# A two-layer graph and expert network on one core: the first layer's slot re-ordered, its routing spread over four slots, and the expert dispatch unrolled

## The chip, the cores and the metric

One Trainium2 chip, one of its cores. The metric is the device time of one execution in microseconds (us). The core has TensorE (PE; its weight loads are listed as PEld), VectorE (DVE), ScalarE (ACT), GpSimd (POOL) and SyncE (SP), which here only issues DMAs.

## The reference, cut to what matters

All numbers are float32. x is 32 batches of 256 nodes with 128 features, adj is 32 x 256 x 256. The change touches the first two of four blocks.

```python
# first graph layer, per batch, H = 4 heads of 32, on n = layernorm(x)
X = lrelu(n @ W_lin + b_lin);  q = lrelu(n @ W_q);  k = lrelu(n @ W_k)
adj_h = adj * sigmoid(q_h @ k_h.T * 32 ** -0.5)          # 256 x 256 for each head
dis   = sum(adj_h, -1) ** -0.5                           # 0 where the degree is 0
x     = x + layernorm(dis * (adj_h @ (dis * X_h))) * ln_g + ln_b
# first expert layer: the two best of 8 experts for each of the 8192 tokens, unweighted
idx = top_k(layernorm(x) @ Wg + bg, 2)
x   = x + sum over the two experts of gelu(n @ W1[e] + b1[e]) @ W2[e] + b2[e]
# then a second graph layer and a second expert layer, which the change leaves as they are
```

## The kernel before

The program is written by hand for all five engines. Every engine runs its own list of instructions in order, and counters (semaphores, `wait_ge`) tie the lists together. Each stage is one function per engine.

**First layer (`gnn0_*`).** A software pipeline over slots `s` from -4 to 40. In slot `s` every engine does a different step for different batches: scores and sigmoid and weighting for batch `s`, keys and queries for `s+1`, transposing x for `s+2`, values for `s-1`, output for `s-2`, and so on back to the gate of the expert layer for `s-6` and `s-7`. The order inside a slot is written out by hand per engine, in the loops at the end of `gnn0_tensor`, `gnn0_scalar`, `gnn0_vector` and `gnn0_gpsimd`.

- PE, per slot: `scores` (L298, 16 matmuls), `transposed_output` (L315), `keys_queries` (L327), `transpose_adj` (L339), `output_rows` (L350), `transpose_x` (L363), `values` (L374, and L375, which adds the bias by a matmul with one row of ones), `transpose_rows` (L387), `degrees` (L398), `gates` (L414), and at the end `transpose_degrees` (L439), which waits for ACT's copy of the degrees (L514).
- ACT: two sigmoids of 1,024 columns (L476), the copies out of PSUM, and last the three normalisations of the slot (L517), for y, x and the rows that go to the experts.
- DVE: two products `adj_h` (L636), the leaky keys and queries (L647), values (L659, L666) and output (L674), six `bn_stats` (L626), the degrees (L679), and a chain of small operations, `solve_steps` (L587 to L620), which finds all reciprocal square roots of the slot: start value, then three Newton steps of three operations (L609, L612, L615), each depending on the last. The other work is put between its links.
- POOL: three additions and products per batch (`add_attention`, L801, L804, L807), then up to four row-scattering DMAs (`send`, L814).

**Routing.** Every fourth slot (10, 14, 18 and so on), DVE picks for four finished batches (1,024 tokens) the two best experts (`choose_steps`, L697 to L724). In the next slot PE counts how many tokens went to each expert before this one: 2 instructions with `before` (L424) and 16 with `ones` (L426), and DVE turns the counts into row numbers (`choose_rows`, L728 to L740). Over the next four slots POOL scatters the 1,024 rows twice (once per chosen expert), 16 indirect DMAs per group, 128 in all. The normalised row carries its token number and the higher expert's rank in two extra columns.

**Dispatch (`ffn0_*`).** When all rows are sent, each expert's rows lie together in DRAM, and 72 blocks of 256 rows are worked off. For each block SP loads the rows (L1004), PE transposes them (L1021), ACT copies (L1076), PE does the hidden layer (L1031), ACT the gelu (L1092), PE the output (L1042), DVE adds the bias (L1158), and POOL scatters the result by token in two indirect DMAs (L1189). DVE also copies the expert's weights to a fixed place (`stage_weights`, L1140) and works out the destinations (L1149, L1152). Which expert a block belongs to is known only at run time, so SP, ACT and DVE read it from memory into a register (`value_load`); DVE does so twice per block. Buffers exist for four blocks. The blocks are done by a loop whose body holds four blocks:

```python
        def over_steps(engine, body):

            body(0, True, False)
            with engine.Fori(1, NBLK // UNROLL - 1) as i:
                body(i, False, False)
            body(NBLK // UNROLL - 1, False, True)
```

SP may load block n+4 when DVE has its destinations (`s_y_at`, `s_higher`) and PE its transposes. DVE does in turn `add_bias(n-2)`, `stage_weights(n+2)`, `destinations(n)`.

Of the kernel before, what the change touches and what calls it, by code (L numbers as in the profile page):

```python
# [41 lines left out]
UNROLL = 4  # L42
DEG_MIN = 2.0 ** -120
RSQRT_MAGIC = float(0x5F3759DF)
# [28 lines left out]
def build_program(nc, I, out):  # L73

    with ExitStack() as ctx:
# [63 lines left out]

        phR = ExitStack()  # L140
# [5 lines left out]
        NROWS = 3  # L146
        rows = sbR("rows", [P, NROWS, GT, ROW])
        xh1T = sbR("xh1T", [P, 2, NN])
        gate = sbR("gate", [P, GT, NE])
# [4 lines left out]
        emask = sbR("emask", [P, GT + 1, NE])  # L154
# [21 lines left out]
        w_k, w_q, w_lin = sb1("w_k", [P, D]), sb1("w_q", [P, D]), sb1("w_lin", [P, D])  # L176
        b_lin = sb1("b_lin", [1, D])
# [17 lines left out]
        AT_X, AT_Y, AT_R = 0, TB, 2 * TB  # L195
        stats = sb1("stats", [P, 2, NLN, 6])
# [3 lines left out]
        rstd = sb1("rstd", [P, 2, NLN + NDEG])  # L200
        shift = sb1("shift", [P, 2, NLN])
        dis = sb1("dis", [P, 2, NDEG])

        s_w1, s_wln = sem("s_w1"), sem("s_wln")
# [3 lines left out]

        s_xhT_ps, s_kq_ps, s_adjT_ps, s_score_ps = sem("s_xhT_ps"), sem("s_kq_ps"), sem("s_adjT_ps"), sem("s_score_ps")
# [4 lines left out]
        s_deg, s_yT, s_yn = sem("s_deg"), sem("s_yT"), sem("s_yn")  # L214
# [4 lines left out]
        s_stats, s_norm, s_dis, s_chA, s_init1 = sem("s_stats"), sem("s_norm"), sem("s_dis"), sem("s_chA"), sem("s_init1")  # L219
# [4 lines left out]
        rank_ps = psum[:, Y_BANK, 0:(GT + 1) * NE]  # L224

        SOLVE_LAG = 3
        FIRST, LAST = -4, NB + 9
# [7 lines left out]
        def solve_no(s):  # L235

            return s + SOLVE_LAG + 1

        def solves(s):
            return batch(s + SOLVE_LAG) or batch(s - 1) or batch(s - 3) or batch(s - 5)  # L240

        def routes(s):

            return s >= 10 and s % GB == 10 % GB and (s - 10) // GB < NG

        def gnn0_sync(sp):
# [20 lines left out]
            for dst, name in ((w_k, "L0_gnn_W_k"), (w_q, "L0_gnn_W_q")):  # L267
                sp.dma_start(dst[:, :], I[name]).then_inc(s_w1, 16)
            load_adj(0)
            sp.dma_start(w_lin[:, :], I["L0_gnn_W_lin"]).then_inc(s_w1, 16)  # L270
            sp.dma_start(b_lin[:, :], I["L0_gnn_b_lin"].rearrange("(a p) -> a p", a=1)).then_inc(s_w1, 16)
            load_x(1)
            load_adj(1)
            for dst, name in ((ln_g, "L0_gnn_ln_g"), (ln_b, "L0_gnn_ln_b")):
                sp.dma_start(dst[:, :], I[name].rearrange("(a n) -> a n", a=1).to_broadcast((P, D)))\
                    .then_inc(s_wln, 16)
            load_adj(2)
            load_gate(sp)
            load_attention3(sp)
            for b in range(NB):  # L280
                if b % 2 == 0 and b // 2 + 2 < NB // 2:
                    load_x(b // 2 + 2)
# [4 lines left out]
        def gnn0_tensor(pe):  # L287
            pe.wait_ge(s_const, 2)
            pe.wait_ge(s_w1, 4 * 16)

# [14 lines left out]
            def transposed_output(b):  # L305
                pe.wait_ge(s_xs, b + 1)
                if b > 4:
                    pe.wait_ge(s_gate, b - 4)
                if b < NB - 4 and b > -4:
                    pe.wait_ge(s_xhT, b + 4)  # L310
                elif b > 0:
                    pe.wait_ge(s_yT, b)
                for c in range(TB):
                    for h in range(HEADS):
                        ins = nc.tensor.matmul(psum[HD * h:HD * (h + 1), YT_BANK, 0:NN],  # L315
                                               xs[:, b % 2, c, HD * h:HD * (h + 1)],
                                               adj_h[:, b % 3, h, c, :], start=(c == 0), stop=(c == TB - 1))
                ins.then_inc(s_yT_ps, 1)

            def keys_queries(b):  # L320
# [122 lines left out]
            for s in range(FIRST, LAST):  # L443
                if batch(s):
                    scores(s)
# [1609 lines left out]
```

## Time and profile before

| | |
|---|---|
| time before, median of 3 runs | 961.0 us (958.96 to 961.82) |
| the profiled execution: its time, its span | 957.8 us, 956.0 us |
| mean granted TensorE clock | 0.856 of full |
| busy: PE, DVE, ACT, POOL | 695.5, 593.8, 431.8, 436.3 us |
| first sigmoid of batch 0, of batch 31 | 18.11 us, 342.48 us |
| first load of an expert block | 436.31 us |
| first and last scatter of expert results | 448.20 us, 692.39 us |

The time is that of the whole execution; the span runs from its first to its last instruction, and every position below is counted from the span's start. Busy shares are means over stages with different limits, so they say little by themselves.

### The profile page before, as it was taken

How to read it: one execution, taken by the hardware profiler on the slowest of the kernel's cores; microseconds unless marked ns; L12 is line 12 of the kernel's file. 1: busy time of each engine (PE TensorE's matmuls, PEld its weight loads, DVE VectorE, ACT ScalarE, POOL GpSimd, SP SyncE). 2: the span in 40 equal slices, each digit the busy share in tenths (PEclk: the TensorE clock that was granted, in tenths of full speed). 3: DMA queues.
4: the chain of work that ended last, by engine and by line, in shares of the span. 5: the costliest groups of instructions: out<-in, count | busy, mean ns of one | idle time of the engine just before them, and what ended most of it. 6: DMA issues, size and time to landing. Idle time of an engine off the chain costs nothing. (4 is left out here: it accounts for less than half of the span.)

```text
span 956.0 us, 18424 instructions
## 1 busy us (share of the span) xinstructions
PE 695.5 (73%) x4886; PEld 543.5 (57%) x4886; DVE 593.8 (62%) x2480; ACT 431.8 (45%) x1018; POOL 436.3 (46%) x478
## 2 busy tenths in 40 slices
PE   3989798888888885405776667676546774699994
PEld 2556565555555553404665556665446673589993
DVE  6898978787878767331333333333267784348898
ACT  4576665565655533103333333332212556567771
POOL 0022245554555557762555555545644310185540
PEclk9998998997898865556889999898768997699998
DMA  7223123222221111822222222222199940102211
GB/s 186 82 63 89 56 78 100 78 80 78 79 78 57 45 35 35 245 87 68 77 77 72 72 83 77 76 72 78 56 216 214 175 110 1 46 1 68 68 36 53
DMA packets 90507, 79.97 MB, mean 84 GB/s; under 512 B 11025, under 2 KB 79810, under 8 KB 89410
## 3 DMA queue, kind: packets, MB, share of 16 engines
q1 hardware_dynamic: 69250, 54.84, 20.5%
q0 software_dynamic: 21184, 24.27, 10.5%
q8 instruction: 33, 0.54, 0.2%
q14 instruction: 40, 0.33, 0.1%
HBM read 46.39 MB, written 32.69 MB: 83 GB/s over the span
## 5 line engine op out<-in xcount | busy, mean ns | idle before, releaser
L1189 POOL DMA_INDIRECT expert_outputs<-y_rows,y_at x144 | 138.5, 962 | 120.8 <-DVE y_rows L1158 77.9
L814 POOL DMA_INDIRECT expert_rows<-rows,row_of x128 | 125.6, 981 | 45.3 <-issue 34.3
L1158 DVE TENSOR_TENSOR y_rows<-psum,f_b 128x256 f32<-128x256 f32 x72 | 30.6, 425 | 124.9 <-PE psum L1042 71.2
L801 POOL TENSOR_TENSOR y_n<-y_n,ln_g 128x256 f32<-128x256 f32 x32 | 23.4, 732 | 185.6 <-ACT y_n L517 185.3
L1092 ACT ACTIVATE hT<-psum,f_b 128x256 f32<-128x256 f32 x144 | 60.5, 471 | 87.6 <-remote 36.7
L1021 PE MATMUL psum<-ident,xin 128*128 128x128 f32 x144 | 33.6, 319 | 90.2 <-DMA xin<-expert_rows 87.8
L1031 PE MATMUL psum<-xinT,wst 128*128 128x256 f32 x288 | 88.2, 434 | 12.1 <-DVE wst L1140 9.9
L1042 PEld LDWEIGHTS psum<-wst,hT 128*128 128x128 f32 x576 | 83.0, 208 | 7.6 <-issue 2.8
L1042 PE MATMUL psum<-wst,hT 128*128 128x128 f32 x576 | 83.2, 292 | 2.5 <-DVE y_rows L1158 2.5
L636 DVE TENSOR_TENSOR adj_h<-psum,adjT 128x1024 f32<-128x1024 f32 x64 | 77.8, 1216 | 9.4 <-ACT psum L476 6.4
L1076 ACT ACTIVATE xinT<-psum 128x256 f32<-128x256 f32 x72 | 27.7, 385 | 116.4 <-PE psum L1021 89.4
L1021 PEld LDWEIGHTS psum<-ident,xin 128*128 128x128 f32 x144 | 17.8, 156 | 99.9 <-issue 69.6
L476 ACT ACTIVATE psum<-psum 128x1024 f32<-128x1024 f32 x64 | 61.3, 994 | 19.4 <-PE psum L298 16.4
L1031 PEld LDWEIGHTS psum<-xinT,wst 128*128 128x128 f32 x288 | 55.3, 213 | 23.5 <-issue 12.6
L1733 PEld LDWEIGHTS psum<-w2s,hT 128*128 128x128 f32 x512 | 61.8, 192 | 4.6 <-ACT hT L1777 2.2
L1715 PE MATMUL psum<-xh3T,w1s 128*128 128x256 f32 x256 | 62.7, 389 | 2.3 <-DVE w1s L1841 1.9
L1733 PE MATMUL psum<-w2s,hT 128*128 128x128 f32 x512 | 62.7, 275 | 2.1 <-DVE xh L1860 2.1
L315 PE MATMUL psum<-adj_h,xs 128*32 128x256 f32 x512 | 44.9, 480 | 22.7 <-issue 20.0
L1324 PE MATMUL psum<-hf,adjT 128*128 128x130 f32 x256 | 38.5, 321 | 23.4 <-issue 13.6
L1140 DVE TENSOR_SCALAR wst<-f_w 128x512 f32 x72 | 32.4, 450 | 33.9 <-issue 33.7
L1777 ACT ACTIVATE hT<-psum,b1sel 128x256 f32<-128x256 f32 x128 | 50.1, 470 | 5.9 <-PE psum L1715 5.8
L1935 POOL COPY w1s<-f_w 128x256 f32 x60 | 24.9, 424 | 60.9 <-issue 32.6
(250 smaller groups left out, 1656.7 us busy)
## 6 DMA issues: line engine op xcount, KB each, us to landing
xin<-expert_rows SPq DMA_DIRECT2D x72, 130.0 KB
adj_in<-in_adj_dram SPq DMA_DIRECT2D x32, 256.0 KB, 3.8
adjT_scratch<-adjT SPq DMA_DIRECT2D x32, 256.0 KB, 3.0
adjT<-adjT_scratch SPq DMA_DIRECT2D x8, 1024.0 KB
xres<-expert_outputs POOLq DMA_DIRECT2D x12, 512.0 KB, 11.3
xres<-in_x_dram SPq DMA_DIRECT2D x16, 256.0 KB, 3.5
out_dram<-yout SPq DMA_DIRECT2D x6, 512.0 KB, 3.1
expert_outputs<-y_rows,y_at POOLq DMA_INDIRECT x144
```

Source lines behind the costliest of these rows:

```text
L315: ins = nc.tensor.matmul(psum[HD * h:HD * (h + 1), YT_BANK, 0:NN], xs[:, b % 2, c, HD * h:HD * (h + 1)], adj_h[:, b % 3, h, c, :], start=( ...
L476: nc.scalar.activation(pair, pair, ACT.Sigmoid, scale=float(HD) ** -0.5).then_inc(s_att, 1)
L636: nc.vector.tensor_tensor(adj_h[:, b % 3, 2 * u:2 * u + 2, :, :].rearrange("p h c n -> p h (c n)"), psum[:, 2 * u:2 * u + 2, :], adjT[:, b ...
L814: pool.indirect_dma_start(rows_dram[:, :], bass.IndirectOffsetOnAxis(ap=row_of[:, g % 3, k, t:t + 1], axis=0), rows[:, g % 3, t, :], None) ...
L1021: ins = nc.tensor.transpose(psum[:, u % 2, r * P:(r + 1) * P], xin[:, u, r, 0:D], ident[:, :])
L1031: ins = nc.tensor.matmul(psum[:, 2 + u, c * SLOTS:(c + 1) * SLOTS], wst[:, u, c * P:(c + 1) * P], xinT[:, u, :], start=True, stop=True)
L1042: ins = nc.tensor.matmul(psum[:, 6 + u % 2, r * P:(r + 1) * P], hT[:, u, c, r * P:(r + 1) * P], wst[:, u, HID + c * D:HID + (c + 1) * D], ...
L1092: ins = nc.scalar.activation(hT[:, u, c, :], psum[:, 2 + u, c * SLOTS:(c + 1) * SLOTS], ACT.Gelu, bias=f0_b1[:, bass.ds(e * FC + c, 1)])
L1189: pool.indirect_dma_start(y_dram[:, :], bass.IndirectOffsetOnAxis(ap=y_at[:, u, r:r + 1], axis=0), y_rows[:, u, r, :], None).then_inc(s_y_ ...
L1715: ins = nc.tensor.matmul(psum[:, 2 * (n % 2) + k, c * NN:(c + 1) * NN], w1s[:, n % SLOTS4, k, c * P:(c + 1) * P], xh3T[:, n * NN:(n + 1) * ...
L1733: ins = nc.tensor.matmul(psum[:, 4 + n % 2, r * P:(r + 1) * P], hT4[:, n % 2, k, c, r * P:(r + 1) * P], w2s[:, n % SLOTS4, k, c * D:(c + 1 ...
L1777: nc.scalar.activation(hT4[:, n % 2, k, c, :], psum[:, 2 * (n % 2) + k, c * NN:(c + 1) * NN], ACT.Gelu, bias=b1sel[:, c, k, n:n + 1]).then ...
```

## The change

It has these parts.

1. **The slot's order** is new on all engines. PE transposes the degrees of batch s-1 after the scores of batch s, and does gates and the adjacency transposes before the keys. ACT puts `normalise_y` between the two sigmoids, and normalises y, x and rows with the numbers solved one slot earlier (`s - 1`), so `rstd`, `shift` and `dis` have three sets in place of two; x is normalised for batch s+3 from statistics taken for batch s+5. The pipeline starts one slot earlier (-5). DVE weighs the values of batch s-2, early in the slot.
2. **Newton**: two steps in place of three, the second one written as a cubic; 8 operations with the start value in place of 10.
3. **Value bias**: the weights are centred once (`w_c = w - mean`), the transposed x gets +1 from ACT's bias, and the bias row is folded into `w_c`, so the matmuls of L375 go.
4. **Routing**: `choose_steps` and the new `place_steps` are spread by single steps over the following slots, and the counting is two matmuls on prefix sums (`upto`) that DVE makes. The last group of four batches is split in two. Sending starts at slot 14. The token column is written by ACT.
5. **Dispatch**: no loop; all 72 blocks are written out. The output bias travels with the staged weights (640 columns in place of 512), so `add_bias` needs no `value_load`; the destinations are one operation, and result rows lie in pairs per token.

```diff
-        SOLVE_LAG = 3
-        FIRST, LAST = -4, NB + 9
+        FIRST, LAST = -5, NB + 9
+        ROUTES = [(GB * g, GB) for g in range(NG - 1)] + [(NB - GB, GB // 2), (NB - GB // 2, GB // 2)]
...
+            nc.tensor.matmul(psum[:, 0, 0:3 * D], ones[:, :], w_all[:, :, :].rearrange("p k d -> p (k d)"),
+                             start=True, stop=False)
+            nc.tensor.matmul(psum[:, 0, 2 * D:3 * D], ones[0:1, :], b_neg[:, :], start=False, stop=True)\
+                .then_inc(s_wc_ps, 1)
...
+            def rank(g, s):
+                nc.tensor.matmul(rank_ps[:, 0:(tiles + 1) * NE], ones[:, :],
+                                 upto[:, 0:tiles + 1, :].rearrange("p t e -> p (t e)"), start=True, stop=False)
+                nc.tensor.matmul(rank_ps[:, 0:tiles * NE], before[:, :],
+                                 emask[:, 4:4 + tiles, :].rearrange("p t e -> p (t e)"), start=False, stop=True)\
+                    .then_inc(s_rank_ps, 1)
...
             for s in range(FIRST, LAST):                      # PE
                 if batch(s):
                     scores(s)
+                if batch(s - 1):
+                    transpose_degrees(s - 1)
+                ranked = ranks(s)
+                if ranked is not None:
+                    rank(ranked, s)
+                if batch(s - 7):
+                    gates(s - 7)
+                if batch(s + 1):
+                    transpose_adj(s + 1)
+                    keys_queries(s + 1, ranked)
                 if batch(s - 2):
                     transposed_output(s - 2)
+                if batch(s - 1):
+                    values(s - 1, ranked)
+                if batch(s + 2):
+                    transpose_x(s + 2)
                 if batch(s - 2):
                     output_rows(s - 2)
                 if batch(s):
                     degrees(s)
                 if batch(s - 6):
+                    transpose_rows(s - 6)
...
             for s in range(FIRST, LAST):                      # ACT
                 if batch(s):
                     sigmoid(s, 0)
+                if batch(s - 4):
+                    normalise_y(s - 4, s - 1)
+                if batch(s):
                     sigmoid(s, 1)
...
+                if batch(s - 6):
+                    normalise_rows(s - 6, s - 1)
+                if batch(s + 3):
+                    normalise_x(s + 3, s - 1)
...
+            for s in range(FIRST, NB + 14):                   # POOL
                 if batch(s - 4):
                     add_attention(s - 4)
+                if batch(s - 14):
+                    send(*parts[s - 14])
...
-        def over_steps(engine, body):
-            body(0, True, False)
-            with engine.Fori(1, NBLK // UNROLL - 1) as i:
-                body(i, False, False)
-            body(NBLK // UNROLL - 1, False, True)
+        def over_blocks(body):
+            for n in range(NBLK):
+                body(n, n % UNROLL, n // UNROLL)
...
-                nc.vector.tensor_scalar(higher[:, u, :], xin[:, u, :, D + 1], expert_rank[:, bass.ds(n, 1)],
-                                        float(NT * P), ALU.is_gt, ALU.mult).then_inc(s_higher, 1)
-                dve.wait_ge(s_higher, n + 1)
-                nc.vector.tensor_tensor(y_at[:, u, :], xin[:, u, :, D], higher[:, u, :], ALU.add).then_inc(s_y_at, 1)
+                nc.vector.scalar_tensor_tensor(y_at[:, u, :], xin[:, u, :, D + 1], expert_rank[:, n:n + 1],
+                                               xin[:, u, :, D], ALU.is_gt, ALU.add).then_inc(s_y_at, 1)
...
+            for n in range(NBLK):                             # DVE
+                if n > 1:
+                    add_bias(n - 2)
+                destinations(n)
+                if n + 2 < NBLK:
+                    stage_weights(n + 2)
```

## Rows read from the trace of the kernel before

**Rows 1.** Windows: stage, length, busy PE, PEld, DVE, ACT, POOL, clock, DMA, GB/s.

```profile
18.11:104.95 86.84, 75.32 (x678) 47.24 (x682) 77.22 (x288) 56.61 (x116) 14.40 (x20) 0.92 0.29 87
104.95:342.48 237.53, 202.22 (x1684) 132.41 (x1676) 192.12 (x747) 137.31 (x291) 120.19 (x139) 0.89 0.24 74
342.48:436.31 93.83, 38.34 (x189) 27.80 (x189) 43.49 (x213) 14.37 (x33) 61.08 (x67) 0.52 0.33 99
...
448.20:693.36 245.16, 170.88 (x972) 146.43 (x970) 82.17 (x278) 80.25 (x205) 138.51 (x144) 0.91 0.25 74
693.36:956.00 262.64, 192.47 (x1297) 177.24 (x1297) 184.55 (x870) 130.79 (x350) 100.40 (x96) 0.88 0.40 90
```

**Rows 2.** Timeline of ACT: sigmoids of batches 11, 12, 13, 16, 17.

```profile
114.64 1.90 ACT L476 ACTIVATE psum<-psum 128x1024 f32<-128x1024 f32 x2
129.85 1.92 ACT L476 ACTIVATE psum<-psum 128x1024 f32<-128x1024 f32 x2 [2.93 <-PE psum L298]
138.90 1.91 ACT L476 ACTIVATE psum<-psum 128x1024 f32<-128x1024 f32 x2
...
172.99 1.93 ACT L476 ACTIVATE psum<-psum 128x1024 f32<-128x1024 f32 x2 [2.36 <-PE psum L298]
184.45 1.91 ACT L476 ACTIVATE psum<-psum 128x1024 f32<-128x1024 f32 x2
```

**Rows 3.** Timeline of DVE and POOL, one slot, from 58.20 us.

```profile
58.20 0.73 POOL L801 TENSOR_TENSOR y_n<-y_n,ln_g 128x256 f32<-128x256 f32 x1 [6.32 <-ACT y_n L517]
58.45 0.52 DVE L587 TENSOR_TENSOR msum<-stats 128x6 f32<-128x6 f32 x1
59.02 0.73 POOL L804 TENSOR_TENSOR y_n<-y_n,ln_b 128x256 f32<-128x256 f32 x1
59.15 0.61 DVE L592 SCALAR_TENSOR_TENSOR mdiff<-mdiff 128x6 f32<-128x6 f32 x1
59.89 0.68 DVE L595 SCALAR_TENSOR_TENSOR veps<-sqsum,mdiff 128x6 f32<-128x6 f32 x1
...
67.11 0.51 DVE L587 TENSOR_TENSOR msum<-stats 128x6 f32<-128x6 f32 x1
```

**Rows 4.** DVE's groups by shape, 60 to 340 us.

```profile
L615 DVE SCALAR_TENSOR_TENSOR rstd<-newt,rstd 128x14 f32<-128x14 f32 x78 | 12.6, 162 | 0.7
...
L685 DVE TENSOR_TENSOR gate<-psum,f_bg 128x16 f32<-128x16 f32 x24 | 3.9, 162 | 0.0
L717 DVE TENSOR_TENSOR emask<-hot 128x64 f32<-128x64 f32 x5 | 3.8, 769 | 0.2
...
L728 DVE TENSOR_TENSOR pos<-psum,filled 128x64 f32<-128x64 f32 x5 | 1.1, 225 | 8.4 <-PE psum L426 8.4
```

**Rows 5.** Timeline at the end of the sending: POOL's last scatter, SP's first loads.

```profile
433.12 0.96 POOL L814 DMA_INDIRECT expert_rows<-rows,row_of  x1 [0.30 <-issue]
...
436.31 3.67 SPq L1004 DMA_DIRECT2D xin<-expert_rows  x4
```

**Rows 6.** DVE's groups by shape, dispatch, 448 to 694 us.

```profile
L1140 DVE TENSOR_SCALAR wst<-f_w 128x512 f32 x68 | 30.5, 449 | 31.1 <-issue 31.1
L1158 DVE TENSOR_TENSOR y_rows<-psum,f_b 128x256 f32<-128x256 f32 x71 | 30.2, 425 | 118.1 <-PE psum L1042 64.3 <-issue 30.5 <-remote 23.3
L1149 DVE TENSOR_SCALAR higher<-xin,expert_rank 128x2 f32<-128x2 f32 x70 | 16.0, 229 | 4.4 <-issue 3.8 <-DMA expert_outputs<-y_rows,y_at 0.6
```

**Rows 7.** Timeline of DVE, dispatch: three successive bias additions.

```profile
524.53 0.42 DVE L1158 TENSOR_TENSOR y_rows<-psum,f_b 128x256 f32<-128x256 f32 x1 [0.76 <-issue]
...
529.82 0.42 DVE L1158 TENSOR_TENSOR y_rows<-psum,f_b 128x256 f32<-128x256 f32 x1 [2.75 <-PE psum L1042]
...
532.13 0.42 DVE L1158 TENSOR_TENSOR y_rows<-psum,f_b 128x256 f32<-128x256 f32 x1 [0.67 <-issue]
```

**Rows 8.** POOL's waits, 448 to 694 us: total, times, longest.

```profile
POOL expert_outputs L1189 <- DVE y_rows L1158: 77.9, 26, 14.1
```

**Rows 9.** DMA queue that fetches instructions, 18 to 383 us: packets, MB, share.

```profile
q8 instruction: 21, 0.34, 0.4%
```

More of the change, by code:

```diff
@@ new lines, in gates @@
+            def gates(b):
+                pe.wait_ge(s_xh1T, b + 1)
+                if b + 8 < NB:
+                    pe.wait_ge(s_xhT, b + 9)
+                elif b + 4 < NB:
+                    pe.wait_ge(s_yT, b + 5)
+                elif b > 0:
+                    pe.wait_ge(s_gate, b)
+                if b == 0:
+                    pe.wait_ge(s_w2, W2_LOADS)
+                    pe.wait_ge(s_const2, CONST2)
+                for t in range(TB):
+                    ins = nc.tensor.matmul(psum[:, YT_BANK, t * NE:(t + 1) * NE], xh1T[:, b % 2, t * P:(t + 1) * P],
+                                           f0_wg[:, :], start=True, stop=True)
+                ins.then_inc(s_gate_ps, 1)
@@ L430, in transpose_degrees, with values @@
-            def transpose_degrees(b, ranked):
+            def values(b, ranked):
+                if ranked is not None and b + 2 >= NB:
+                    pe.wait_ge(s_ranked, ranked + 1)
+                elif b + 2 < NB:
+                    pe.wait_ge(s_raw, b + 3)
+                elif b > 0:
+                    pe.wait_ge(s_xd, b)
+                for t in range(TB):
+                    ins = nc.tensor.matmul(psum[:, KQ_BANK, t * P:(t + 1) * P], xhT[:, b % 4, t * P:(t + 1) * P],
+                                           w_c[:, 2, :], start=True, stop=True)
+                ins.then_inc(s_X_ps, 1)
@@ L744, in gnn0_vector @@
                 steps = solve_steps(s) if solves(s) else iter(())
-                picks = choose_steps((s - 10) // GB) if routes(s) else iter(())
+                late = s >= NB
+                next(steps, None)
+                if s == FIRST + 1:
+                    dve.wait_ge(s_wc_ps, 1)
+                    nc.vector.scalar_tensor_tensor(
+                        w_c[:, :, :].rearrange("p k d -> p (k d)"), psum[:, 0, 0:3 * D], -1.0 / D,
+                        w_all[:, :, :].rearrange("p k d -> p (k d)"), ALU.mult, ALU.add).then_inc(s_wc, 1)
+                if batch(s - 2):
+                    weigh_values(s - 2)
+                next(picks, None)
+                if batch(s - 2):
+                    leaky_values(s - 2)
                 next(steps, None)
@@ L1033, in hidden, with output @@
                 ins.then_inc(s_bh_ps, 1)
-            def output(i, u, first):
-                n = UNROLL * i + u
+            def output(n):
+                u = n % UNROLL
                 pe.wait_ge(s_bh, n + 1)
-                if not (first and u < 2):
+                if n > 1:
                     pe.wait_ge(s_y_rows, n - 1)
@@ L1179, in ffn0_vector @@
[L1179 to L1193 removed]
+            stage_weights(0)
```

703 lines of the change are left out of this document (357 added, 346 removed).

## The prediction

> **What bounds the kernel now.** I read the windows by stage first, then the timeline of one slot, then the groups and waits of the two stages that the change touches.
>
> The first layer takes 86.84 us for slots 0 to 9 and 237.53 us for slots 10 to 30; its tail and the rest of the sending take 93.83, the dispatch 245.16 and all that follows 262.64 [rows 1]. The first two stages belong to DVE: it is busy 77.22 of 86.84 us, and in slot 5 it issues without a gap, from one start of its chain (58.45) to the next (67.11), 8.66 us [rows 3]. From slot 10 on DVE is busy only 192.12 of 237.53 us [rows 1]. The loss sits in the routing. An ordinary slot takes 138.90 - 129.85 = 9.05 us; the slot with the counting takes 129.85 - 114.64 = 15.21, and the one after it, seen in the next group, 184.45 - 172.99 = 11.46 [rows 2].
>
> The tail is POOL's. One scatter costs 0.96 + 0.30 = 1.26 us [rows 5]; after the additions of the last batch 36 are still to be sent, and SP loads the first block 2.2 us after the last one ends (434.08 to 436.31) [rows 5].
>
> In the dispatch POOL has 2 x 1.26 = 2.52 us of work per block. The stage takes 245.16 / 72 = 3.41 us per block, and POOL waits 77.9 us in it for the biased rows [rows 1, 8]. DVE in its turn is idle 118.1 us before adding the bias [rows 6]. Its fastest round is 532.13 - 529.82 = 2.31 us, and the round before that took 5.29 [rows 7]. So the block rate is POOL's pace plus bubbles in a ring of four buffers, where DVE at 2.31 us is hardly faster than POOL and can't catch up after one.
>
> **The change part by part.** The sum is made against the profiled execution, 957.8 us with a span of 956.0; it lies 3.2 us under the median of 961.0, which I add at the end.
>
> *A slot of the first layer.* I start from slot 5 (8.66 us), which has no statistics of finished rows and no gates. Those are two `bn_stats` and one small operation, an estimate of 0.5 us from the spacing of such operations: 9.2 us, which the ordinary slot's 9.05 agrees with. From this go:
>
> - POOL's three operations. DVE's small operations at 58.45, 59.15 and 59.89 take 0.52, 0.61 and 0.68 us, and each of the first two ends where POOL's operation ends (58.93, 59.75) [rows 3]. Undisturbed such an operation takes 0.16 [rows 4]. That is 0.36 + 0.45 + 0.52 = 1.3 us per slot. The change starts POOL's batch after ACT's first sigmoid, when DVE is in the two 1.2 us products whose one input is in PSUM. No row shows a product against a POOL operation; the nearest is the gate addition, also from PSUM, which lies at that place in the slot and still takes 162 ns [rows 4]. So I take the delay as gone, with 0 and 1.3 us as bounds.
> - Two links of the Newton chain, 0.2 us each from start to start where nothing is between them (0.16 to 0.17 of it busy) [rows 4]: 0.4 us.
>
> That leaves 7.5. The PE work removed (bias matmuls, 16 of the counting instructions) I cost at nothing inside the slot: DVE covers it. It matters where DVE waited for the counts, 8.4 us in five groups [rows 4], which I count as gone, since the two matmuls come early in the slot and DVE has the values to weigh meanwhile.
>
> Routing adds 20 DVE operations per group in place of 21. Back to back one costs about 0.25 us, in the shadow of the chain's links 0.14; 4.0 us per group, 1.0 per slot, bounds 0.7 and 1.3. Some of them stood beside POOL at 769 ns each [rows 4] and no longer do. Slot: 8.5 us without a wait.
>
> DVE idles 45.4 us in slots 10 to 30 [rows 1]; without the counts' 8.4 that is 37, or 1.8 per slot. PE no longer ends its slot by waiting for ACT's degrees, which takes the wait for them; the delay after the start of a new group's scatters (the 11.46 us slot) I can't place, and leave. I keep half: 0.9. The slot comes to 9.4 us, bounds 8.5 and 10.3. Slots 10 to 30: 21 x 9.4 = 197 against 237.5, **-40 us** (-59 to -21).
>
> *Slots 0 to 9.* Six of them have POOL's 1.3, all have the 0.4: 11.8 us, if all of it counts. The first slots wait for ACT and PE instead (9.6 us idle in the stage [rows 1]), so **-8 us** (-12 to 0).
>
> *The start.* Three weights, the bias, a matmul and one DVE operation now precede the first keys, and DVE's first wait is for all four loads. I see about two DMA issues and one matmul more ahead of the first sigmoid: **+1.5 us** (0 to +3).
>
> *The tail.* Sending begins two slots later, so after the last addition 44 scatters are left, not 36: 8 x 1.26 = 10 us more. What it gives back: the routing of the last groups no longer holds up the slots before it, and POOL no longer waits for the last rows, as the last group is half as large. POOL's own work from slot 31 on is five batches of 3 x 0.81 us and 60 scatters of 1.26, 88 us; with about 1.5 us until slot 31's rows, 1.5 more as that slot is longer than POOL's work in it, and the 2.2 us at the end, 93 us. Before it is 93.8: **-1 us** (-4 to +5). This is the queue to watch: everything else in the tail (experts' weights, row table, padding) is hidden behind POOL's 44 scatters, 55 us.
>
> *The dispatch.* DVE's round loses one `value_load` (0.75 us, an estimate from the idle stretches of rows 6 and 7: 0.76 us before the bias addition) and one of two destination operations with its wait (0.26); the weight copy grows by 640/512 of 449 ns, +0.11 [rows 6]. 2.31 becomes 1.4 us, well under POOL's 2.52. PE, ACT and SP lose their register arithmetic. Destinations are now ready before the weight copy, so SP's next load starts about 0.9 us sooner. POOL is then the bound at 2.52, and the question is how much of the remaining 0.89 us per block stays as bubbles. The late bias additions (5.29 us) come from waits whose cause I can't see; with a ring of four at POOL's pace (10.1 us) and some 8 us of latency from load to bias, part of each is absorbed. I take 2.9 us per block: 72 x 0.51 = **-36 us** (bounds 2.6 and 3.3: -58 to -8). Nothing after the dispatch changes in work: 262.64 us stay [rows 1].
>
> Sum: -40 - 8 + 1.5 - 1 - 36 = -83.5; 961.0 - 83.5 = 877.5, say 877 us.
>
> **Two rules beside this.** The trace shows DVE's small operations ending with POOL's [rows 3]. The Trainium skill, SBUF — State Buffer, Who interferes with whom, gives the cause: an operation with two inputs in SBUF needs a port that POOL holds exclusively, one with a PSUM input does not. By that rule the products are free, but the leaky keys and the routing steps, with two SBUF inputs, could be hit at their new places; this is the rival on the port below. On unrolling, the same skill's Runtime: NRT & Kernel Launch, Instruction fetch mechanics, says that a sequencer refills in 16 KiB blocks ahead of need and that a taken branch outside its window stalls; here the loop's body is small, so that rule alone gives the unrolling little.
>
> **Rivals.**
>
> 1. *Bubbles stay.* If the delays in the dispatch hit POOL's own supply chain whatever DVE's pace, the block stays at 3.4 us. For it: DVE's waits are longest for PE, whose work per block is unchanged. Against: DVE's fastest round is now slower than needed to catch up. 877 + 36 = 913 us.
> 2. *POOL at its floor and slots without waits.* 2.6 us per block and slots of 8.8: 877 - 22 - 13 = 842 us. POOL's even scatters in the tail [rows 5] speak for the floor.
> 3. *The port.* POOL's third operation, or all three, falls on DVE operations with two SBUF inputs: 0.5 us in each of 31 slots, 893 us. For it: the products cover only 2.3 us and POOL's work of 2.4 starts later than they do.
> 4. *The order gains nothing.* PE now puts the keys behind the values' weighing and the counts (`s_xd`, `s_ranked`), and behind the keys stand the output, values, x and degrees. If this chain takes the time that the routing left, the slots stay at 11.3 us and only the dispatch gains: 877 + 48 = 925 us.
> 5. *Slower.* 72 blocks written out must be fetched: PE alone has some 32 instructions per block. If each of about 20 extra fetches stopped an engine that all wait for, it would take 84 / 20 = 4.2 us each to cancel the gain; at 5 us each the time is 977. Against: 21 such fetches lie in the first layer [rows 9], where DVE issues without a gap for a whole slot [rows 3].
>
> **How the numbers follow.** Forecast 0.42 (its own range 855 to 905), rival 1 0.20, rival 2 0.16, rival 3 0.08, rival 4 0.07, rival 5 0.05, no gain anywhere 0.02. The range reaches to rivals 2 and 4: 838 to 926. A measurement of this kernel tells a change from none at about 0.3%, 3 us: faster 0.93, within that 0.02, slower 0.05.
>
> **What would show it.** First sigmoids of batches 12 to 30 evenly 9.4 us apart, with no slot over 12; DVE's L587, L592, L595 counterparts at 0.16 to 0.17 us; no wait of DVE for the counts over 1 us; batch 31's sigmoid near 296 us, the first block load near 389, POOL issuing without a gap over the 44 scatters before it. In the dispatch, scatters 1.26 us apart for long runs and a stage near 209 us. The prediction is wrong if the slots wait for PE's keys, if POOL still waits over 40 us in the dispatch, or if the tail grows by the 10 us of its extra scatters.

## The result, and the profile after

The changed kernel takes 926.1 us (923.5 to 929.2, 4 runs), the kernel before beside it 961.4: a ratio of 0.9635 (0.9598 to 0.9673). It is faster by 35 us where I had forecast 84, and lies at the very top of my range, 0.1 us above its 926. Its profiled execution has a span of 924.7 us. Windows by stage of the changed kernel (columns as in rows 1):

```profile
20.89:92.39 71.50, 62.43 (x639) 39.20 (x640) 67.14 (x262) 56.88 (x114) 13.47 (x18) 1.00 0.35 106
92.39:316.79 224.40, 175.21 (x1536) 109.97 (x1536) 168.95 (x710) 139.21 (x295) 114.93 (x131) 0.87 0.23 73
316.79:425.78 108.99, 27.30 (x143) 18.00 (x143) 44.18 (x233) 16.10 (x39) 69.59 (x75) 0.52 0.29 90
...
437.00:661.05 224.05, 160.86 (x976) 143.28 (x974) 72.98 (x208) 81.20 (x205) 143.22 (x144) 0.92 0.30 82
661.05:924.70 263.65, 193.36 (x1297) 177.93 (x1297) 184.45 (x870) 130.90 (x350) 100.69 (x97) 0.87 0.40 89
```

| stage, us | before | after | change | forecast |
|---|---|---|---|---|
| start, to the first sigmoid | 18.11 | 20.89 | +2.8 | +1.5 |
| slots 0 to 9 | 86.84 | 71.50 | -15.3 | -8 |
| slots 10 to 30 | 237.53 | 224.40 | -13.1 | -40 |
| tail, to the first block load | 93.83 | 108.99 | +15.2 | -1 |
| first load to first result scatter | 11.89 | 11.22 | -0.7 | 0 |
| dispatch | 245.16 | 224.05 | -21.1 | -36 |
| rest | 262.64 | 263.65 | +1.0 | 0 |

Three stages miss by 27, 16 and 15 us to one side, one by 7 to the other. In slots 10 to 30 DVE has less work than before (168.95 us for 192.12 [rows 1]) and yet is idle for 55.5 us, where it was idle for 45.4. Where does that idle time lie? DVE's groups by shape, 60 to 310 us, changed kernel (busy, mean ns, idle before and what ended it):

```profile
L642 DVE SCALAR_TENSOR_TENSOR mdiff<-mdiff 128x6 f32<-128x6 f32 x25 | 13.5, 539 | 0.0
...
L637 DVE TENSOR_TENSOR msum<-stats 128x6 f32<-128x6 f32 x25 | 4.2, 170 | 3.3
L744 DVE TENSOR_SCALAR veps<-psum 128x8 f32<-128x8 f32 x25 | 4.1, 164 | 25.1 <-PE psum L479 20.7 <-remote 4.3
...
L817 DVE TENSOR_TENSOR pos<-psum,filled 128x64 f32<-128x64 f32 x5 | 1.1, 215 | 0.0
```

The wait for the counts is gone (L817; 8.4 us before [rows 4]). In its place stand 25.1 us before the degrees (L744), for PE. The timeline around one change of slot shows why PE is late. It is the changed kernel's, from 226 us:

```profile
226.34 0.69 PE L479 MATMUL psum<-ident,deg 128*128 128x128 f32 x2 [2.86 <-ACT deg L555]
227.06 0.17 DVE L744 TENSOR_SCALAR veps<-psum 128x8 f32<-128x8 f32 x1 [2.82 <-PE psum L479]
...
228.38 0.85 POOL L914 TENSOR_TENSOR y_n<-y_n,ln_g 128x256 f32<-128x256 f32 x1 [3.70 <-ACT y_n L558]
228.56 0.69 DVE L642 SCALAR_TENSOR_TENSOR mdiff<-mdiff 128x6 f32<-128x6 f32 x1
...
229.25 2.34 DVE L700 TENSOR_TENSOR adj_h<-psum,adjT 128x1024 f32<-128x1024 f32 x2
...
234.45 0.44 PE L454 MATMUL psum<-ident,rows 128*128 128x128 f32 x2
...
236.95 0.38 ACT L549 ACTIVATE xh1T<-psum 128x256 f32<-128x256 f32 x1 [1.89 <-remote]
237.23 0.38 ACT L555 ACTIVATE deg<-psum 128x256 f32<-128x256 f32 x1
237.49 1.03 ACT L515 ACTIVATE psum<-psum 128x1024 f32<-128x1024 f32 x1
```

PE ends the transposes of the rows (L454) at 234.89. ACT has nothing else to do and waits for them, but copies them (L549) only at 236.95: the increment by which PE tells ACT arrives 2.0 us after the work that it reports. Behind it stand ACT's copy of the degrees, PE's transpose of them (L479), DVE's next step and the next sigmoid. In the slots that send rows, the profile puts 28.8 us of ACT's idle time before L549 down to "remote", that is, to no work of an engine. The group of L549, changed kernel, 127 to 317 us:

```profile
L549 ACT ACTIVATE xh1T<-psum x17: 372/384/385, 134.0 to 315.2; 128x256 f32<-128x256 f32 x17
its engine sat idle before it (us, times) until:
  remote: 28.8, 11
```

The trace also holds the increments one by one, so the delay can be read without the idle times. In the slots before the scatters each stands at most 0.07 us behind the end of the instruction that makes it, most of them 0.01 us. In slots 10 to 30 of the changed kernel 73 increments stand more than 0.5 us behind the last instruction that could have made them, up to 3.5 us, all of them PE's and all later than the first scatter (131.91 us). In its dispatch there are 110, up to 4.0 us, all PE's. The kernel before has them too: 38 in slots 10 to 30 and 108 in the dispatch. After the last scatter of the dispatch neither kernel has one. Such an increment is called late below.

The tail shows the same on other engines. Timeline of the changed kernel, 398 to 426 us:

```profile
398.25 24.65 SPq L1103 DMA_DIRECT2D expert_rows<-pad_rows  x8
...
401.79 0.17 DVE L1217 COPY end_b<-end_a 128x2 f32<-128x2 f32 x1 [2.57 <-remote]
...
404.61 0.36 DVE L1217 COPY end_a<-end_b 128x4 f32<-128x4 f32 x1 [2.59 <-remote]
...
410.64 1.15 POOL L930 DMA_INDIRECT expert_rows<-rows,row_of  x1 [0.30 <-issue]
...
425.78 0.41 SPq L1113 DMA_DIRECT2D xin<-expert_rows  x1
```

POOL sends its last row at 410.64, without one gap in the 44 scatters, as forecast. But SP needs 24.65 us to issue eight padding transfers (9.17 us in the kernel before), and goes on to the first load only 14 us after POOL's end. Until 417.5 us one instruction of SP starts every 1.4 us, so the effect outlasts POOL's last scatter (over at 411.79) by 5.8 us. Even DVE's steps that wait only for DVE's own last step begin up to 2.6 us after it.

In the dispatch it is DVE that waits for PE again. POOL's waits for DVE, 73.7 and 1.9 us, look like the 77.9 before [rows 8], but both totals hold the wait for the first block, which ends where the stage begins: 25.2 us after and 14.1 before. Inside the stage POOL waits 50.4 us for DVE where it waited 63.8, and 30.5 us between its own instructions (`issue`) where it was 42.8. That is 25.7 us less, beside 4.7 us more of scattering (143.22 for 138.51), and makes the stage's 21 us. (The line names the destinations, `y_at`; those of a block are long ready then, and it is the result rows of L1255 that end the wait.) DVE's and POOL's waits, changed kernel, 437 to 661 us (total, times, longest):

```profile
DVE y_rows L1255 <- PE psum L1151: 86.2, 34, 3.5
DVE y_rows L1255 <- issue: 17.5, 10, 2.6
```

```profile
POOL expert_outputs L1277 <- DVE y_at L1249: 73.7, 43, 25.2
POOL expert_outputs L1277 <- issue: 30.5, 100, 0.3
POOL expert_outputs L1277 <- DVE y_rows L1255: 1.9, 1, 1.9
```

### The profile page after: what moved, and what is told of

Read it like the earlier page. It is cut to its first block and busy times, and to the rows that moved or that the text cites. A ratio compares the mean times of both kernels' runs of the same rounds, so it can differ in the third digit from the quotient of the medians.

```text
span 924.7 us, 16632 instructions
## 1 busy us (share of the span) xinstructions
PE 636.0 (69%) x4654; PEld 500.0 (54%) x4654; DVE 554.2 (60%) x2375; ACT 436.6 (47%) x1026; POOL 443.6 (48%) x478
## 3 DMA queue, kind: packets, MB, share of 16 engines
q0 software_dynamic: 21184, 24.27, 11.2%
## 5 line engine op out<-in xcount | busy, mean ns | idle before, releaser
L1277 POOL DMA_INDIRECT expert_outputs<-y_rows,y_at x144 | 143.7, 998 | 106.0 <-DVE y_at L1249 73.7
L1140 PE MATMUL psum<-xinT,wst 128*128 128x256 f32 x288 | 84.8, 421 | 54.0 <-issue 46.4
L914 POOL TENSOR_TENSOR y_n<-y_n,ln_g 128x256 f32<-128x256 f32 x32 | 25.4, 794 | 170.6 <-ACT y_n L558 170.6
L1255 DVE TENSOR_TENSOR y_rows<-psum,wst 128x256 f32<-128x256 f32 x72 | 30.4, 422 | 118.9 <-PE psum L1151 92.0
L700 DVE TENSOR_TENSOR adj_h<-psum,adjT 128x1024 f32<-128x1024 f32 x64 | 75.0, 1212 | 0.4 <-ACT psum L515 0.3
L515 ACT ACTIVATE psum<-psum 128x1024 f32<-128x1024 f32 x64 | 64.3, 1010 | 14.5 <-PE psum L334 9.7
L1130 PE MATMUL psum<-ident,xin 128*128 128x128 f32 x144 | 30.6, 298 | 46.6 <-DMA xin<-expert_rows 46.3
L408 PE MATMUL psum<-xhT,w_c 128*128 128x256 f32 x128 | 46.7, 500 | 16.5 <-DVE xd L725 15.7
L2024 POOL COPY w1s<-f_w 128x256 f32 x60 | 24.9, 426 | 59.0 <-issue 30.5
L1804 PEld LDWEIGHTS psum<-xh3T,w1s 128*128 128x128 f32 x256 | 47.3, 195 | 8.0 <-DVE w1s L1930 2.1
L1240 DVE TENSOR_SCALAR wst<-f_w 128x640 f32 x72 | 36.2, 503 | 25.2 <-issue 24.9
```

The costliest lines, as they stand in the source:

```text
L408: ins = nc.tensor.matmul(psum[:, KQ_BANK, n * NN:(n + 1) * NN], w_c[:, n, :], xhT[:, b % 4, :], start=True, stop=True)
L515: nc.scalar.activation(pair, pair, ACT.Sigmoid, scale=float(HD) ** -0.5).then_inc(s_att, 1)
L700: nc.vector.tensor_tensor(adj_h[:, b % 3, 2 * u:2 * u + 2, :, :].rearrange("p h c n -> p h (c n)"), psum[:, 2 * u:2 * u + 2, :], adjT[:, b ...
L1140: ins = nc.tensor.matmul(psum[:, 2 + u, c * SLOTS:(c + 1) * SLOTS], wst[:, u, c * P:(c + 1) * P], xinT[:, u, :], start=True, stop=True)
L1277: pool.indirect_dma_start(y_dram[:, :], bass.IndirectOffsetOnAxis(ap=y_at[:, u, r:r + 1], axis=0), y_rows[:, u, r, :], None).then_inc(s_y_ ...
L1804: ins = nc.tensor.matmul(psum[:, 2 * (n % 2) + k, c * NN:(c + 1) * NN], w1s[:, n % SLOTS4, k, c * P:(c + 1) * P], xh3T[:, n * NN:(n + 1) * ...
```

## The experiments

Twelve kernels ran in four calls, on three chips; the kernel before ran beside each, and its time turned out to be the first finding.

| call | chip | before, us | kernels |
|---|---|---|---|
| 1 | Q | 876.9 (870.2 to 884.1) | e1, e2, e3, e4 |
| 2 | R | 951.7 (942.3 to 953.9) | e5, e6 |
| 3 | R | 950.1 (946.0 to 955.3) | e7, e8, e9, e10 |
| 4 | S | 956.9 (1 run) | e11, e12 |

**e1_sp_early**, on chip Q, adds one wait in `store_adjT`:

```diff
                 sp.wait_ge(s_adjT, b + 1)
+                sp.wait_ge(s_att, 2 * b + 1)
```

> The changed kernel with one more wait on SP: the store and the load of an adjacency go out only after the first sigmoid of the next slot, when POOL does its additions and no scatter is under way. In the changed kernel the slots 14 to 31 take 11.1 us each, and in them PE's increments reach ACT 2 to 4 us late just after SP has issued its transfers among POOL's scatters. Theory A (the transfers beside the scatters hold the increments up): the late increments go, these slots fall to about 9 us, and the kernel gains some 30 us. Theory B (the scatters alone hold them up): slots stay at 11 us, total within 5 us of 926. Theory C (the new order of the slot is itself 11 us long): no change of the slots either, and PE's increments may come in time without anything being gained.

832.3 us, 0.948 of before (0.939 to 0.956). The slots 14 to 30 take 8.70 us each. That looks like theory A; it is not, as e4, which lacks this edit, and e6 show.

**e2_send_last**, on chip Q, moves all `send` calls behind the loop over the slots and has nine row buffers.

> The changed kernel with nine row buffers, and POOL sends no row before all 32 batches have been added: the slots run without a scatter, and 128 scatters of 1.26 us (161 us) follow them. Read are the slots 14 to 31 alone; the total must rise by about 60 to 70 us. If scatters hold up the signals (theories A and B), these slots take 8.1 to 8.6 us, as slots 10 to 12 do in the changed kernel, and no increment of PE comes late. If the new order is 11 us long by itself (theory C), they stay near 11 us.

932.1 us, one run; slots 14 to 30 at 8.4 us each. On this chip it tells nothing of late increments, as the slots with scatters (e1, e4) take no more than 8.7 and the 128 scatters behind the slots make none late either. It is repeated as e11.

**e3_before_unrolled**, on chip Q, is the kernel before with

```diff
-            body(0, True, False)
-            with engine.Fori(1, NBLK // UNROLL - 1) as i:
-                body(i, False, False)
-            body(NBLK // UNROLL - 1, False, True)
+            for i in range(NBLK // UNROLL):
+                body(i, i == 0, i == NBLK // UNROLL - 1)
```

> The kernel before with its 72 blocks written out and nothing else changed: DVE keeps both register reads and both destination operations. My prediction gave the unrolling itself nothing and the thinner DVE round 36 us. If that holds, the dispatch stays at 3.4 us per block (245 us) and the total at 961. If the loop's register arithmetic on all engines was the brake, the block falls towards the 3.1 us of the changed kernel and the total to about 940. If fetching the written-out code costs, it is slower than 961.

876.0 us, 0.996 of before (0.990 to 1.002): unrolling alone gives nothing. Windows of it: slots 0 to 9, slots 10 to 30, tail, dispatch, rest.

```profile
18.06:103.66 85.60, 73.09 (x678) 46.65 (x682) 76.72 (x288) 56.68 (x116) 14.40 (x20) 0.94 0.29 90
103.66:321.42 217.76, 190.60 (x1684) 127.56 (x1676) 189.17 (x746) 136.97 (x290) 119.72 (x139) 0.93 0.26 80
321.42:407.48 86.06, 35.39 (x189) 25.77 (x189) 45.16 (x214) 14.25 (x34) 60.66 (x67) 0.56 0.36 108
...
419.15:604.70 185.55, 150.17 (x972) 132.63 (x970) 87.75 (x278) 83.52 (x205) 139.61 (x144) 0.98 0.33 99
604.70:871.85 267.15, 196.68 (x1297) 181.13 (x1297) 184.78 (x870) 131.01 (x350) 100.80 (x97) 0.85 0.39 88
```

Its dispatch runs at 185.55 / 72 = 2.58 us per block, close to POOL's 2.52, with the thick DVE round of 2.31 us that I had blamed.

**e4_wide_rows**, on chip Q, loads a block in longer pieces; its first layer is the changed kernel's, line for line.

```diff
-  rows_dram[bass.ds(at, SLOTS), :].rearrange("(t p) d -> p t d", p=P)
+  rows_dram[bass.ds(at, SLOTS), :].rearrange("(p t) d -> p t d", p=P)
```

> The changed kernel, but a block's load gives each partition two neighbouring rows (1,040 bytes in a piece) in place of two rows 128 apart (520 bytes each): the same bytes in half as many pieces; which row lies in which partition does not matter, as each row carries its token. If the number of pieces in flight beside the scatters makes the stretches in which no increment arrives (three of about 1.2 us in every three blocks), the block falls from 3.1 us towards 2.8 and the total by about 20 us. If the scatters alone make them, or the time of the load doesn't matter, it stays within 3 us of 926.

830.2 us, 0.946 of before (0.937 to 0.955). Windows of the same stages:

```profile
20.44:91.69 71.25, 61.98 (x639) 39.05 (x640) 67.10 (x262) 56.84 (x114) 13.46 (x18) 1.00 0.35 107
91.69:272.87 181.18, 158.25 (x1531) 99.93 (x1532) 167.51 (x709) 139.16 (x295) 114.22 (x129) 0.95 0.28 89
272.87:366.44 93.57, 25.10 (x149) 17.54 (x149) 45.13 (x235) 16.09 (x39) 71.18 (x77) 0.57 0.34 107
...
377.40:561.75 184.35, 148.36 (x976) 131.37 (x974) 77.48 (x208) 83.44 (x205) 140.75 (x144) 0.99 0.34 100
561.75:826.90 265.15, 194.87 (x1297) 179.37 (x1297) 184.85 (x870) 130.77 (x350) 99.73 (x97) 0.87 0.40 89
```

The group of L549 in it, 125 to 273 us, no longer knows a "remote":

```profile
L549 ACT ACTIVATE xh1T<-psum x17: 371/383/384, 131.8 to 271.8; 128x256 f32<-128x256 f32 x17
its engine sat idle before it (us, times) until:
  PE psum L454: 2.6, 8
```

DVE's idle time in slots 10 to 30 is 13.7 us, not 55.5. On chip Q no increment of any engine comes late, in any stage of e1 to e4. Whether the edits or the chip did that, the next call tells.

**e5_after_again**, on chip R, is the changed kernel itself.

> The changed kernel itself, unchanged, beside the kernel before on the chip of this call. In the runs on record so far the kernel before took 961 us in the first measurement and 877 beside the first four experiments, and there no increment of PE came late, with or without scatters. Theory S (the late signals belong to the chip or to what runs beside it, not to the kernel): where the kernel before takes about 877, the changed one takes about 832, its dispatch stands at 2.55 us per block like that of the kernel before, and the slots 14 to 31 at 8.8; where the kernel before takes about 961, the changed one takes 926 with late increments. Theory K (the earlier load and the shifted transfers of the other experiments removed them): 926 either way, with late increments in its trace.

908.6 us, 0.958 of before (0.950 to 0.965); 212.57 us for slots 10 to 30, 219.55 for the dispatch, late increments throughout. With e1 to e4 that speaks for theory S. That theory names the chip or what runs beside the kernel; with one call on Q and two on R the runs can't tell these two apart.

**e6_both**, on chip R, joins the edits of e1 and e4.

> The changed kernel with both edits of the first call: adjacency transfers after the slot's first sigmoid, and a block's load in pieces of 1,040 bytes. On a chip where no increment comes late I expect no difference from the changed kernel (within 3 us), since the dispatch stands at POOL's 2.55 us per block and the slots wait for no transfer. On a chip where they come late, this is the first run of either edit there: by theory A (transfers beside scatters make it) the slots fall from 11.1 to about 9 us and the block from 3.1 to about 2.8; by theory B (nothing of the kernel's transfers matters) neither moves.

918.5 us, 0.965 of before (0.957 to 0.973): no better than e5. Windows of e6, slots 10 to 30 and dispatch:

```profile
92.37:310.26 217.89, 175.93 (x1536) 108.68 (x1536) 168.15 (x710) 139.21 (x296) 115.00 (x131) 0.87 0.25 76
428.90:648.50 219.60, 160.73 (x976) 143.29 (x974) 73.58 (x208) 81.07 (x205) 142.81 (x144) 0.93 0.29 84
```

Theory A falls, for both edits: neither another place for SP's transfers of the adjacency nor a load in fewer pieces makes the slots or the blocks faster.

**e7_ring6**, on chip R, with `RING = 6`; the result rows and destinations (`y_rows`, `y_at`) get six buffers too:

```diff
-        xin = sb2("xin", [P, UNROLL, SLOTS // P, ROW])
+        xin = sb2("xin", [P, RING, SLOTS // P, ROW])
...
-                    sp.wait_ge(s_y_at, n - UNROLL + 1)
+                    sp.wait_ge(s_y_at, n - RING + 1)
```

> The changed kernel with six buffers in place of four for the rows that come in, the result rows and their destinations; weights, hidden layer and PSUM banks stay at four. Where signals come late in the dispatch, POOL then has up to two more blocks of results to scatter while nothing arrives: if the stretches without a signal (4 to 6 us in every 9.4 us) are only ridden out in the ring, the block falls from 3.05 us to about 2.7 and the total by 20 to 25 us. If each stretch also stops POOL's own supply whatever lies in the ring (my rival 1), it stays at 3.0 to 3.1. Where no signal comes late, nothing changes: 2.55 us per block.

913.8 us, 0.959 of before (0.954 to 0.965), beside 0.962 for e10: no difference. The block takes 3.06 us, 3.05 in e10. More room for loads and for results gains nothing. That leaves the handovers between PE, ACT, PE and DVE as the place where the time goes, each made by an increment; the buffers between those (weights, hidden layer, PSUM) stayed at four, and no run tried more of them.

**e8_send_first**, on chip R, puts `send` ahead of `add_attention` in POOL's slot.

> The changed kernel, POOL doing the four scatters of a slot ahead of the three additions instead of behind them. The same scatters fall in the first half of the slot, under DVE's products and PE's keys, and the signals at the slot's end (degrees, rows) go out when no scatter is under way. Where signals come late: if only those at the end of the slot cost time, since each of PE, ACT, PE, DVE then waits for the last, the slots 14 to 31 fall from 10.5 or 11 us to about 9.5. If any four scatters cost the slot 2.5 us wherever they lie, they stay. Where none comes late: slots at 8.8 us, unless POOL's additions, now later, hold up the rows' statistics (then up to 1 us more per slot).

920.1 us, 0.969 of before (0.966 to 0.971). Slots 10 to 30 take 224.24 us against 212.01 in e10, and DVE still waits 25.0 us for the degrees from 140 to 310 us. Moving the scatters helps nothing: 75 increments come late in its slots 10 to 30, 63 in e10's.

**e9_before_unrolled_again**, on chip R, is e3 once more.

> The kernel before with only its 72 blocks written out, once more, in the hope of a chip on which signals come late (the first run of it met none: 2.57 us per block). There it separates the two parts of the dispatch: if DVE's thinner round is what brought the block from 3.39 to 3.05 or 3.11 us, this kernel stays at 3.4; if unrolling did, it is at 3.1. Where no signal comes late, 2.57 again.

948.6 us, 0.998 of before (0.994 to 1.001). Unrolling gives nothing here either. The dispatch in the windows of e9:

```profile
443.37:681.00 237.63, 167.17 (x972) 146.65 (x970) 81.45 (x278) 80.62 (x205) 137.62 (x144) 0.90 0.27 78
```

**e10_after_third**, on chip R, is the changed kernel as the measure for the three above.

> The changed kernel unchanged, as the measure for the other three on this chip. With the kernel before at about 877 I expect 831 here, dispatch 2.55 us per block, slots 10 to 30 in about 181 us and no late signal; with the kernel before at 950 to 961, 908 to 926.

914.5 us, 0.962 of before (0.957 to 0.967). Slots 10 to 30 and the dispatch in the windows of e10:

```profile
91.94:303.95 212.01, 169.78 (x1536) 106.67 (x1536) 165.31 (x710) 139.03 (x296) 115.83 (x131) 0.90 0.25 78
...
421.96:641.60 219.64, 157.73 (x976) 140.43 (x974) 73.01 (x208) 80.89 (x205) 143.35 (x144) 0.94 0.30 84
```

237.63 against 219.64: where increments come late, what the change does to the dispatch beside unrolling it is worth 18 us. DVE's thinner round is the largest part of it by my costs; no run separates it from the earlier destinations and loads.

**e11_send_last_again**, on chip S, is e2 once more.

> The changed kernel with all scatters after the slots, once more (the first run of it met no late signal at all and its slots 18 to 30 took 8.5 us). On a chip where signals come late (the kernel before at 945 us or more): if they need scatters in flight, the slots 10 to 30 again take 178 us in place of the changed kernel's 212 to 224, and late increments appear only once the scatters begin. If the transfers of the adjacency alone are enough on such a chip, the slots stay near 10 us.

974.0 us, one run, beside 956.9 for the kernel before. Slots 10 to 30 in its windows:

```profile
92.07:270.36 178.29, 158.32 (x1531) 99.63 (x1532) 165.15 (x709) 138.56 (x295) 46.93 (x63) 0.95 0.22 67
```

178.29 us, and not one late increment before the scatters begin at 303.5 us; from there to the first load there are 24, and in its dispatch, which scatters, 108 (219.79 us). So the order of the slot is not what takes 10 to 11 us.

**e12_plain**, on chip S, sends the same rows to fixed places, and loads the blocks and writes their results at fixed places too. It leaves out the sorting by expert, so it computes something else.

```diff
-                    pool.indirect_dma_start(
-                        rows_dram[:, :], bass.IndirectOffsetOnAxis(ap=row_of[:, g % NROWS, k, t:t + 1], axis=0),
-                        rows[:, g % NROWS, t, :], None).then_inc(s_sent[g % NROWS], 16)
+                    pool.dma_start(rows_dram[at:at + P, :], rows[:, g % NROWS, t, :])\
+                        .then_inc(s_sent[g % NROWS], 16)
```

> The changed kernel with every scatter of POOL replaced by a plain transfer of the same 128 rows from the same queue to a fixed place; blocks are loaded from fixed places as well. It leaves out the sorting of the rows, so the rows that the experts see and the order of their results are others. Both stages run with the same bytes, loads and instructions on PE, ACT and DVE. On a chip where signals come late: if the scattered addresses or the per-row descriptors that POOL writes for them make the signals late, they vanish here, the slots fall to about 8.5 us and the block to 2.5 us or less, since POOL's plain issue is shorter than 1.26 us. If any write from POOL's queue beside SP's transfers does it, slots and blocks keep their 10.5 and 3.05 us.

769.4 us, one run, beside 956.9. Slots 10 to 30, tail and dispatch in its windows:

```profile
93.38:271.98 178.60, 158.07 (x1531) 99.29 (x1532) 165.00 (x709) 138.86 (x296) 83.05 (x131) 0.95 0.32 92
271.98:348.16 76.18, 25.43 (x149) 17.64 (x149) 44.75 (x235) 16.10 (x39) 42.94 (x75) 0.55 0.59 129
359.36:505.35 145.99, 139.69 (x976) 130.23 (x974) 72.95 (x208) 83.58 (x205) 86.58 (x144) 1.00 0.45 126
```

No increment is late in any stage, on the chip where e11, in the same call, has them from its first scatters on. Each of the two kernels ran there once. POOL's transfers go through the same queue in the same number of packets with the same bytes. This is the line of that queue in e12, and then in the changed kernel:

```profile
q0 software_dynamic: 21184, 24.27, 14.5%
```

```profile
q0 software_dynamic: 21184, 24.27, 11.2%
```

## Why the prediction was wrong, point by point

**The step that failed** is the reading of idle time in the kernel before. I saw it (37 us of DVE's idle time in slots 10 to 30, 118 us in the dispatch), wrote that I could not see its cause, and still took part of it as something that the change would remove: "I keep half: 0.9" in the slot, 2.9 us per block. What stayed was more: DVE idles 55.5 / 21 = 2.6 us per slot, where e4 leaves 13.7 / 21 = 0.7, and the block takes 224.05 / 72 = 3.11 us, where e4 takes 2.56. What stayed are mainly late increments, and the experiments tie them to POOL's scatters on some chips: none without scatters (e11), none with plain transfers (e12), none on chip Q even with scatters (e3, e4). The change keeps all 272 scatters. In slots 10 to 30 it even has more late increments than the kernel before, 73 and 38. The timeline suggests why, as four handovers in a row (PE, ACT, PE, DVE) now lie at the slot's end beside the scatters; but e8, which moves the scatters away, gains nothing, so that this is the reason is not shown.

Chip Q serves as the same comparison without them, e3 for before (0.996 of it) and e4 for after. That e4 stands for the changed kernel is an assumption: its one edit lies in the block's load, and the same edit together with e1's gains nothing on chip R (e6).

| stage, us | e3 | e4 | change | forecast |
|---|---|---|---|---|
| slots 0 to 9 | 85.60 | 71.25 | -14.4 | -8 |
| slots 10 to 30 | 217.76 | 181.18 | -36.6 | -40 |
| tail | 86.06 | 93.57 | +7.5 | -1 |
| dispatch | 185.55 | 184.35 | -1.2 | -36 |

So the forecast of 84 us holds on no chip: the whole kernel gains 46 us on Q (876.0 to 830.2), and 35, 43 and 36 us in the first measurement and the two calls on R. Where increments come late, the change doesn't remove the loss; where they don't, the dispatch has none to remove.

- *The slot.* Without sending or routing I had 7.5 us; slot 5 takes 7.3 and slots 7 to 9 take 7.4 (slot 6 takes 8.7). With routing 8.5; e4 has 181.18 / 21 = 8.63, e11 178.29 / 21 = 8.49. That half of the mechanism was right in the mean, but the slots are not even, as I had them: in e11 every fourth takes 10.5 us and the others 7.4 to 8.1. The 0.9 for waits was too much on chip Q and too little elsewhere (224.40 / 21 = 10.69). That -36.6 on chip Q comes so near to -40 is partly luck, as e3 is there 0.9 us per slot faster than the kernel that I forecast from, and e4 0.8 faster than my 9.4.
- *POOL's operations.* Two are out of DVE's way (L637, L646 at 0.17 and 0.15 us), but the first still meets L642, at 539 ns for 0.16: 0.38 us per slot stay of the 1.3. In the timeline L642 starts at 228.56, in POOL's operation of 228.38 to 229.23, and ends with it. That is a small piece of my rival 3. By the rule on ports in the Trainium skill (SBUF — State Buffer, Who interferes with whom) a DVE operation with two inputs in SBUF is held up by a POOL operation that reads SBUF, and one with an input in PSUM is not. The trace agrees: L642 is of the first kind, and the two products from 229.25 on (L700), of the second, take 2.34 us beside POOL's other two operations, no more than the 1.21 us of each elsewhere.
- *Slots 0 to 9* were mis-sized: I cut the gain to 8 us for waits on ACT and PE in the first slots, and it was 15.3 (14.4 on chip Q).
- *The tail.* The 44 scatters were right, and so was the 93 us for the tail after where no increment is late (93.57 in e4). It is longer than before by 7.5 us there, where I had balanced it to -1. The miss is on the other side of the subtraction: the tail before is 93.83 in the first measurement and 86.06 on chip Q, and I had taken the difference for POOL's work and for a wait that goes. It was there to be read (the row behind this list): in the kernel before PE ends the counts of the last group (L426) at 400.48, and DVE goes on with them only at 412.08, 11.6 us later. It waits 15.15 us there, and 3.59 at the same place on chip Q (e3). On the chip of the first measurement SP's padding came on top. I had called it hidden behind the scatters; it ran into 14 us.
- *The dispatch.* That unrolling gives nothing was right (e3, e9). That DVE's round is what limits the block was wrong on chip Q, where both kernels stand at POOL's pace, and right in part on chip R: 18 us of the 36. The 77.9 us that I read as POOL's wait in the stage held 14.1 us from before it; my sign that the prediction is wrong, over 40 us of waiting, is met all the same (50.4). Rival 1 names the mechanism best, but had the block at 3.4 us where it came to 3.11.
- *Rival 4* comes out at nearly the measured time (925 us), and that is luck: it has the new order keep the slots at 11 us, and e4 and e11 run that order in 8.6 and 8.5.

DVE's wait for the counts, timeline of the kernel before, from 412 us:

```profile
412.08 0.22 DVE L728 TENSOR_TENSOR pos<-psum,filled 128x64 f32<-128x64 f32 x1 [15.15 <-remote]
```

**What stays open.** Why a scatter delays increments on some chips and not on others, and by which path, no run shows; nor whether it is the chip itself or its state at that hour. Nor was the changed kernel itself timed on chip Q. None of the versions that compute the same beats it beyond the intervals where increments come late; e4 and e1 were the fastest on chip Q, with no changed kernel beside them.

## What to carry to other kernels

Idle time whose end the profile puts down to "remote", or to an engine that had ended microseconds before, need not be slack that a better order wins back: look for what else is running in just those stretches (here scatters), and forecast with that term kept. And time the old kernel on more than one chip: it moved by 9% here, which is more than the change did.

## What the runs showed of the hardware

- While POOL scatters rows, PE's increments come late, in bunches: one per slot, and one about every 9.4 us in the dispatch, up to 3.5 and 4.0 us behind the work that they report (changed kernel, first measurement); one in the tail of the kernel before came 11.6 us late. In the tail an instruction of SP started only every 1.4 us from 396 to 418 us, and a small DVE operation that waits only for the one before it on DVE came up to 2.6 us after it. Late increments and the 1.4 us came on R (e5), S (e11) and the first measurement's chip, and not on Q; the kernel before takes 950 to 961 us on the former and 877 on Q.
- A plain transfer of 128 rows from POOL occupies it for 0.54 us (e12) where a scatter of the same rows takes 0.96 and 0.30 more. With it the block falls to 145.99 / 72 = 2.03 us and the kernel to 769 us. By the ratio 0.96 of chip R the changed kernel would take 956.9 x 0.96 = 919 us on chip S, so scattering rather than plain sending costs some 150 us there (an estimate). About 80 to 90 of these are what goes with late increments, as e4 with scatters and no late increment takes 830 us on Q; the rest is POOL's longer time per scatter (an estimate too, from runs on different chips). The Trainium skill (DMA: Bandwidth & Descriptors, SWDGE vs HWDGE vs iDMA) has POOL's software write the descriptors of direct and indirect transfers alike to rings in SBUF; the runs agree in that both appear in one queue with the same 21,184 packets, and if both are written to the rings in the same way, that writing alone can't be what makes the increments late.
